# An eight-layer attention stack on one NeuronCore: Wo and W2 products formed token-major at once, biases added from PSUM by VectorE, and another order of work at the opening

## The reference: what is computed

```python
for i in range(B):                       # B = 8 layers, H*K = 1024, F = 1024
    residual = x
    Q = _feature_map(jnp.einsum('nsd,hdk->nshk', x, Wq[i]) + bq[i])   # elu(x) + 1
    Kf = _feature_map(jnp.einsum('nsd,hdk->nshk', x, Wk[i]) + bk[i])
    V = jnp.einsum('nsd,hdk->nshk', x, Wv[i]) + bv[i]
    KV = jnp.sum(Kf * V, axis=1)
    sumK = jnp.sum(Kf, axis=1)
    Z = 1.0 / (Q * sumK[:, None] + 1e-06)
    att = Q * KV[:, None] * Z
    y = jax.nn.gelu(att.reshape(n, s, H * K) @ Wo[i] + bo[i])
    x = _layer_norm(y + residual, ln1_s[i], ln1_b[i])
    residual = x
    h = jax.nn.gelu(x @ W1[i] + b1[i])
    h = jax.nn.gelu(h @ W2[i] + b2[i])
    x = _layer_norm(h + residual, ln2_s[i], ln2_b[i])
```

## Time and profile before

| | us |
|---|---|
| median of 3 runs | 3186.2 (3174.65 to 3186.39) |
| the profiled execution | 3182.43 |
| its span, first to last instruction | 3180.7 |
| TensorE busy (matmuls) | 2953.2 |
| VectorE busy | 2327.8 |
| ScalarE busy | 1890.1 |
| GpSimd busy | 921.6 |

### The profile page before, as it was taken

How to read it: one execution, slowest core, us unless ns; L and a number is a source line. 1 busy time by engine, 2 the same in 40 slices (tenths; PEclk the granted TensorE clock), 3 DMA queues, 4 the chain that set the end, 5 groups by cost and what they waited for, 6 DMA issues and landing times. The chain is left out here.

```text
span 3180.7 us, 36072 instructions
## 1 busy us (share of the span) xinstructions
PE 2953.2 (93%) x11560; PEld 2010.1 (63%) x11561; DVE 2327.8 (73%) x3334; ACT 1890.1 (59%) x2824; POOL 921.6 (29%) x590
## 2 busy tenths in 40 slices
PE   4799999999999999999999999999999969988895
PEld 3566666666656665666666666666666536766563
DVE  7778888888787879788878788878888627752111
ACT  3666677667767776776677667766776614432221
POOL 5004231523151315131513151315131123323002
PEclk8899999999999999999999999999999989988998
DMA  5001101100011001100100010001100010013212
GB/s 128 1 1 23 29 5 32 27 27 17 19 26 27 17 19 26 27 17 20 26 27 17 20 25 27 17 20 26 27 17 4 1 53 1 0 37 134 81 45 76
DMA packets 212241, 92.90 MB, mean 29 GB/s; under 512 B 146792, under 2 KB 207984, under 8 KB 212048
## 3 DMA queue, kind: packets, MB, share of 16 engines
q1 hardware_dynamic: 209408, 83.30, 10.3%
q0 software_dynamic: 2640, 7.21, 0.7%
HBM read 80.24 MB, written 10.22 MB: 28 GB/s over the span
## 5 line engine op out<-in xcount | busy, mean ns | idle before, releaser
L341 PE MATMUL PS<-XTHI,WHI 128*128 128x512 f32 x1536 | 655.0, 426 | 64.5 <-DVE EX L641 44.7
L343 PE MATMUL PS<-XTHI,WLO 128*128 128x512 f32 x1536 | 613.6, 399 | 0.0
L342 PE MATMUL PS<-XTLO,WHI 128*128 128x512 f32 x1536 | 613.3, 399 | 0.0
L269 POOL TENSOR_TENSOR RSTD<-MV,EPS 128x4 f32<-128x4 f32 x68 | 41.2, 606 | 1539.3 <-DVE MV L713 1531.0
L391 PE MATMUL Y<-H,W2S 128*128 128x512 f32 x1024 | 458.1, 596 | 2.7 <-DVE R L703 2.7
L391 PE MATMUL Y<-ATT,WO 128*128 128x512 f32 x1024 | 451.7, 594 | 4.1 <-ACT ATT L540 2.7
L540 ACT ACTIVATE ATT<-INV,CC,CE 128x128 f32<-128x128 f32 x1024 | 425.1, 481 | 3.8 <-DVE INV L687 3.8
L341 PEld LDWEIGHTS PS<-XTHI,WHI 128*128 128x128 f32 x1536 | 294.5, 192 | 157.2 <-issue 67.8
L505 ACT ACTIVATE EX<-PS,BNEG 128x512 f32<-128x512 f32 x256 | 169.9, 686 | 309.5 <-PE PS L343 307.1
L342 PEld LDWEIGHTS PS<-XTLO,WHI 128*128 128x128 f32 x1536 | 294.6, 192 | 83.7 <-issue 20.3
L391 PEld LDWEIGHTS Y<-ATT,WO 128*128 128x128 f32 x1024 | 194.6, 190 | 226.2 <-issue 215.0
(11 more groups left out here) (189 smaller groups left out, 4737.9 us busy)
## 6 DMA issues: line engine op xcount, KB each, us to landing
STAGE<-L_attn_Wk SPq DMA_DIRECT2D x128, 64.0 KB, 2.1
STAGE<-L_attn_Wv SPq DMA_DIRECT2D x128, 64.0 KB, 2.1
STAGE<-L_attn_Wq SPq DMA_DIRECT2D x128, 64.0 KB, 2.1
WO<-L_attn_Wo SPq DMA_DIRECT2D x8, 1024.0 KB, 5.3
W2S<-L_attn_W SPq DMA_DIRECT2D x8, 1024.0 KB, 5.4
STAGE<-L_attn_W SPq DMA_DIRECT2D x64, 128.0 KB, 3.6
RAW<-L_ffn_r_gate SPq DMA_DIRECT2D x8, 512.0 KB
RAW<-L_ffn_r_up SPq DMA_DIRECT2D x8, 512.0 KB
```

What stands on the lines that cost most here:

```text
L341: nc.tensor.matmul(out, whi[:, kc, :], xhi[:, kc, :], start=(kc == 0), stop=False)
L342: nc.tensor.matmul(out, whi[:, kc, :], xlo[:, kc, :], start=False, stop=False)
L343: ins = nc.tensor.matmul(out, wlo[:, kc, :], xhi[:, kc, :], start=False, stop=(kc == KD - 1))
```

## The change

1. `down` swaps its operands. The activations are loaded as stationary operand, 128 tokens at a time, and the 256 columns of the weights stream past. The product has tokens on the partitions at once, in four blocks of 128 tokens. Its blocks are issued (0, 2), (1, 3) for Wo and (0, 1), (2,), (3,) for W2.
2. `to_tm` and its two uses are gone.
3. The biases now lie along the free axis. They are loaded as one row of 256 broadcast to all partitions (`load_row`, in place of `load_fm`). VectorE adds them while it reads `Y` (`biased`, semaphores `y_b` and `z_b`), into `T`.
4. ScalarE's GELU works in place on `T`, one instruction of 128x1024. For y it stands where it stood; for z it stands behind the first hidden GELU. The residual reads `T`.
5. VectorE's addition for y stands between the sums and the tables of pair 1. That for z stands in the sums of pair 3, behind `hidden_lo`. The buffer waits of TensorE (`res1`, `res2`) become `y_b` and `z_b`.
6. At the opening, VectorE makes the low part of the first input before the statistics of the others, and does the normalisations one tile at a time, each behind a pair's tables. GpSimd does the square roots of tiles 1 to 3 together, and waits for the first normalised tile before it splits weights.

The core of the diff, all in `attention_stack` (TensorE, ScalarE, VectorE in this order; the buffers, the loads with `load_row` and the semaphores are left out):

```diff
-            def to_tm(done, value, transposed):
-                pe.wait_ge(done, value)
-                for b in range(TS):
-                    for kc in range(KD):
-                        ins = nc.tensor.transpose(Ytm[:, b, kc * P:(kc + 1) * P], T[:, kc, b * P:(b + 1) * P],
-                                                  ident[:, :])
-                ins.then_inc(transposed, 1)
-            def down(w, src, m, chunks):
-                for c in chunks:
-                    ins = nc.tensor.matmul(Yfm[:, m, :], w[:, c, m * P:(m + 1) * P], src[:, c, :],
-                                           start=(c == 0), stop=(c == HC - 1))
+            def down(w, src, blocks, chunks=range(HC)):
+                for b in blocks:
+                    for c in chunks:
+                        ins = nc.tensor.matmul(Ytm[:, b, :], src[:, c, b * P:(b + 1) * P], w[:, c, :],
+                                               start=(c == 0), stop=(c == HC - 1))
...
                 pair(0, 0, 2, 1)
                 if tile:
                     if at_least(l, t, 2):
-                        pe.wait_ge(res2, g - 1)
+                        pe.wait_ge(z_b, g - 1)
                     if tt == 0:
                         pe.wait_ge(wo_in, (tl + 1) * 16)
                     pe.wait_ge(att, g * PAIRS + 3)
-                    down(WO, ATT, 0, range(HC - 2))
+                    down(WO, ATT, (0, 2), range(HC - 2))
                     pe.wait_ge(att, g * PAIRS + 4)
-                    down(WO, ATT, 0, range(HC - 2, HC))
+                    down(WO, ATT, (0, 2), range(HC - 2, HC))
                 pair(1, 0, 2, 1)
                 if tile:
-                    down(WO, ATT, 1, range(HC)).then_inc(y_mm, 1)
-                pair(2, 0, 2)
-                if tile:
-                    to_tm(y_act, g + 1, yt_mm)
-                pair(2, 1)
+                    down(WO, ATT, (1, 3)).then_inc(y_mm, 1)
+                pair(2, 0, 2, 1)
                 if before:
                     if tile:
-                        pe.wait_ge(res1, g + 1)
+                        pe.wait_ge(y_b, g + 1)
                     else:
-                        pe.wait_ge(res2, g - 1)
+                        pe.wait_ge(z_b, g - 1)
                     if zt == 0:
                         pe.wait_ge(w2_in, (zl + 1) * 16)
                     pe.wait_ge(h_act, g * HC)
-                    down(W2S, H, 0, range(HC))
+                    down(W2S, H, (0, 1))
                 pair(3, 0, 2, 1)
                 if before:
-                    ins = down(W2S, H, 1, range(HC - 3 if tile else HC))
+                    down(W2S, H, (2,))
+                    ins = down(W2S, H, (3,), range(4 if tile else HC))
...
                     if before:
-                        ins = down(W2S, H, 1, range(HC - 3, HC))
+                        ins = down(W2S, H, (3,), range(4, HC))
...
                     hidden(tl, tt, g)
-                if before:
-                    to_tm(z_act, g, zt_mm)
...
-            def gelu_down(mm, bias, bias_in, done, l, t, value):
-                if t == 0:
-                    act.wait_ge(bias_in, (l + 1) * 16)
-                act.wait_ge(mm, value)
-                for m in range(KD):
-                    ins = nc.scalar.activation(T[:, m, :], Yfm[:, m, :], ACT.Gelu_apprx_tanh, bias=bias[:, m:m + 1])
-                ins.then_inc(done, 1)
-            def hidden(l, t, g, between):
+            def gelu_down(biased, done, value):
+                act.wait_ge(biased, value)
+                nc.scalar.activation(T[:, :, :], T[:, :, :], ACT.Gelu_apprx_tanh).then_inc(done, 1)
+            def hidden(l, t, g, between, before):
...
+                    if m == 0 and before:
+                        gelu_down(z_b, z_act, g)
...
                 if tile:
-                    gelu_down(y_mm, BO, bo_in, y_act, tl, tt, g + 1)
+                    gelu_down(y_b, y_act, g + 1)
...
-                if before:
-                    zl, zt = slot_of(l, t - 1)
-                    gelu_down(z_mm, B2, b2_in, z_act, zl, zt, g)
+                if before and not tile:
+                    gelu_down(z_b, z_act, g)
                 if exists(l, t + 2):
                     input_hi(g + 2)
                 if tile:
-                    hidden(tl, tt, g, (nl, nt, 2) if more else None)
+                    hidden(tl, tt, g, (nl, nt, 2) if more else None, before)
...
+                if biased2 is not None:
+                    z_biased(*biased2)
...
+            def biased(mm, value, bias, bias_in, layer, t, free, done):
+                if t == 0:
+                    dve.wait_ge(bias_in, (layer + 1) * 16)
+                if free is not None:
+                    dve.wait_ge(*free)
                 dve.wait_ge(mm, value)
-                nc.vector.tensor_tensor(R[:, w, :, :], Ytm[:, :, :], add, ALU.add).then_inc(res, 1)
+                nc.vector.tensor_tensor(T[:, :, :], Ytm[:, :, :], bcast(bias[:, :], TS), ALU.add).then_inc(done, 1)
+            def residual(w, value, gelu, add, res):
+                dve.wait_ge(gelu, value)
+                nc.vector.tensor_tensor(R[:, w, :, :], T[:, :, :], add, ALU.add).then_inc(res, 1)
...
+            def z_biased(l, t, g, tile):
+                zl, zt = slot_of(l, t - 1)
+                biased(z_mm, g, B2, b2_in, zl, zt, (res1, g + 1) if tile else (res2, g - 1), z_b)
...
                 if old:
-                    residual(w, g - 1, zt_mm, R[:, w, :, :], res2)
+                    residual(w, g - 1, z_act, R[:, w, :, :], res2)
                     statistics(w, g - 1, mv2, res2, 1)
                 if tile:
                     newton(tl, tt, 3)
@@ -743,11 +750,15 @@
                     newton(nl, nt, 0)
                     features(nl, nt, 1)
                     sums_of(nl, nt, 1)
+                if tile:
+                    biased(y_mm, g + 1, BO, bo_in, tl, tt, (res2, g - 1) if old else None, y_b)
+                if more:
                     denominators(nl, nt, 1)
                 if tile:
                     if old:
                         dve.wait_ge(xn, g - 1)
-                    residual(w, g + 1, yt_mm, X[:, tt * TS:(tt + 1) * TS, :], res1)
+                    residual(w, g + 1, y_act, X[:, tt * TS:(tt + 1) * TS, :], res1)
...
-                    sums_of(nl, nt, 3)
+                    sums_of(nl, nt, 3, biased2=(l, t, g, tile) if before else None)
...
             norm_input(0)
+            input_lo(0)
             input_statistics(1)
-            input_lo(0)
             input_statistics(2)
             input_statistics(3)
-            for t in range(1, TILES):
-                norm_input(t)
-            slot(0, -1)
+            for p in range(PAIRS):
+                features(0, 0, p)
+                sums_of(0, 0, p)
+                denominators(0, 0, p)
+                if p < TILES - 1:
+                    norm_input(p + 1)
+                if p < PAIRS - 1:
+                    newton(0, 0, p)
+            input_lo(1)
```

GpSimd at the opening:

```diff
             for k in range(HC):
-                if k % 2 == 0:
-                    t = k // 2
-                    bs = slice(t * TS, (t + 1) * TS)
-                    rstd(RSTD0[:, bs], MV0[:, bs, 1], EPS0, mv0, 2 * t + 2, r0, t + 1)
+                if k == 0 or k == 2:
+                    for t in range(TILES)[:1] if k == 0 else range(1, TILES):
+                        bs = slice(t * TS, (t + 1) * TS)
+                        rstd(RSTD0[:, bs], MV0[:, bs, 1], EPS0, mv0, 2 * t + 2, r0, t + 1)
+                if k == 0:
+                    pool.wait_ge(x0, 1)
```

More of the change, by code:

```diff
@@ L80, in attention_stack @@
         BUP = sb("BUP", [P, 3, HC])
-        BO = sb("BO", [P, KD])
+        BO = sb("BO", [P, D])
         B1 = sb("B1", [P, HC])
-        B2 = sb("B2", [P, KD])
+        B2 = sb("B2", [P, D])
         LN1P = sb("LN1P", [P, 2, D])
@@ L123, in attention_stack @@
             sem(n) for n in ("bo_in", "b1_in", "b2_in", "wo_in", "w2_in", "ln1_in", "ln2_in"))
-        k_mm, v_mm, q_mm, y_mm, yt_mm, x1t_mm, h_mm, z_mm, zt_mm, xt_mm = (
-            sem(n) for n in ("k_mm", "v_mm", "q_mm", "y_mm", "yt_mm", "x1t_mm", "h_mm", "z_mm", "zt_mm", "xt_mm"))
+        k_mm, v_mm, q_mm, y_mm, x1t_mm, h_mm, z_mm, xt_mm = (
+            sem(n) for n in ("k_mm", "v_mm", "q_mm", "y_mm", "x1t_mm", "h_mm", "z_mm", "xt_mm"))
         b_neg, clipped, ex, log, inv, y_act, x1_hi, h_act, z_act, xt_hi = (
@@ L132, in attention_stack @@
             sem(n) for n in ("snap", "kf", "wq", "kv_mul", "sums", "stat", "denom", "residue", "recip", "xt_lo", "x1_lo"))
-        res1, mv1, x0, n1, res2, mv2, n2, mv0 = (
-            sem(n) for n in ("res1", "mv1", "x0", "n1", "res2", "mv2", "n2", "mv0"))
+        y_b, res1, mv1, x0, n1, z_b, res2, mv2, n2, mv0 = (
+            sem(n) for n in ("y_b", "res1", "mv1", "x0", "n1", "z_b", "res2", "mv2", "n2", "mv0"))
         half_set, w_hi, w_lo, r1, r2, xn_s, xn, r0 = (
@@ L185, in load_ln, with load_row @@
```

(17 more changed lines are left out.)

13 lines of the change are left out of this document (6 added, 7 removed).

## The result

The changed kernel takes **3246.1 us** (median of four runs, 3239.0 to 3251.4), the kernel before 3182.7 beside it (3174.7 to 3186.4): ratio 1.020, 95% interval 1.018 to 1.021. The forecast was 3237 with a range of 3174 to 3265, and "slower" had 0.66. The profiled execution has a span of 3249.8 us, against 3180.7 before; the spans are 69.1 us apart.

A forecast was written before the change was run, and what follows sets the result against it. The kernel was taken as balanced: a slot is as long as TensorE's work and as a VectorE-ScalarE chain. 3182.4 + 49 (middle stretch) + 2 (quiet slots) + 10 (clock) - 6 (opening) = 3237 us; range 3174 to 3265.

The forecast's parts named there:

- slower: Whole kernel: time beyond the within-0.5% band, which reached to 3202 us; chance 0.66.
- The middle stretch: End of pair 1's sums to pair 2's features: 11.1 us every slot, +49 over seven layers, +2 for two quiet slots.
- my estimate by that page: ScalarE's table switch, now on the chain: by the page another 1.4 us on 30 slots, result near 3280.
- Transposes worth nothing: TensorE: removing 64 groups of eight transposes, 66.4 us busy time, gains nothing because the chain does not pass through TensorE.
- products for nothing: TensorE: twice as many products, half as wide, cost nothing; two at 0.442 us against one at 0.447.
- Addition and GELU of z: VectorE's b2 addition behind X1LO and ScalarE's GELU are hidden by existing waits: nothing; uncovered, up to 2.3 us a slot.
- Cover under X1LO: TensorE idles about 2 us before input's transposes; lower clock costs 1.5 us in a third of slots: +10, between 0 and +40.
- the head follows TensorE: Rival: without the transposes each slot starts 0.85 us earlier, taking back 26 us, to 3201; chance 0.18.
- Opening: Kernel start: spread normalisations start pair 0's features near 27.6, pair 3's near 81 to 84; -6, between 0 and -15.
- The checks: Expected trace signs: TensorE busy time down some 60 us, quiet slots 76.8 us, longest of a layer near 86.
- TensorE is the bound: Rival: VectorE and ScalarE run ahead, slots shrink by TensorE's work, 38 us, to 3138, up to 3165; chance 0.14.
- The change gives only its opening: Rival: both waits fall on free places, leaving only the opening's -6, 3176 us; chance 0.06.

The follow-up runs named there:

- run 1: Changed kernel with VectorE's addition of y's bias moved ahead of the reduction in the sums of pair 1; 3175.4 us, ratio 0.997.
- Run 7: Changed kernel with VectorE's addition of y's bias moved later, behind the tables of pair 1; 3291.3 us, ratio 1.034.
- run 3: Changed kernel with z's eight transposes put back at each slot's end, results unused; 3245.1 us, ratio 1.019.
- run 8: Changed kernel with six instead of four W2 products behind the turning of x1; 3208.6 us, ratio 1.009.
- run 4: Changed kernel with the old order of work at the opening put back on VectorE and GpSimd; 3251.1 us, ratio 1.021.
- run 6: Kernel before the change, with one W2 product instead of three behind the turning of x1, the other two issued ahead; 3224.0 us, ratio 1.013.

## Why the prediction was right, and where it was not

**The middle stretch, +49 and +2: right, and its reason is shown.** I worked out 11.1 us from durations of the trace before; it measured 11.0 (11.4 in one slot of four). The sum is +49.6 against +51. Runs 1 and 7 moved only the addition, and the stretch went to 8.1 and 13.1. ScalarE's wait turned from the product to VectorE, 7.5 to 7.8 us in three slots of four, where I had said some 8 (10.5 in the fourth). The switch of tables is on the chain now, and still takes 1.28 us, with the next activation 0.02 us behind it (1100.32 to 1101.62). The Trainium skill, "ScalarE: Activation LUTs" (What ACT_TABLE_LOAD costs), adds a drain to each load; my estimate by that page was near 3280. The drain does not show in this trace either.

**Transposes worth nothing, products for nothing: right.** Run 3 puts half of the transposes back, those of z, and the time stays; those of y were not put back. The products cost 5.8 us of 910.

**Addition and GELU of z: nothing.** Both stand behind X1LO, in the third part of the slot. In the quiet slots that are not struck this part lasts 45.0 or 46.3 us, against 45.2 or 46.4 before, so they add nothing there, and TensorE's products into Y wait 1.4 us for additions in the whole kernel (first row of L388 above).

**Cover under X1LO, +10: the mechanism was right, the size was off.** This is the term that was mis-sized. The wait is 2.07 us as predicted, and a struck slot loses 1.64 us by run 8, where I took 1.5. But "if a third of 30 slots pay, less the three that already do", 7 slots, came from three in seven of the earlier trace rows, where the wait is another one. Measured are 21 less 3, 18 slots: 18 x 1.64 = **+29.6**. The forecast came near all the same, in part by luck, because something that it did not contain went the other way: the third part grew by 23.0 only, so the rest of it got 6.6 us shorter. By the traces 4.5 of these 6.6 us lie in the longest slots of six layers (316.2 us in all before, 311.7 in run 8, where no slot is struck), the rest in 0.1 to 0.2 us a slot. That has the sign of my rival "the head follows TensorE", which gave 26, but not its size; and run 3 speaks against its reason, since with z's transposes back the part is as long as in the change. What makes it 6.6 shorter stays open.

**Opening, -6: a little less.** 4.3 us at the first turning of x1, by run 4; the time itself, 5 us, is within the scatter. The features began at 27.31, as worked out (27.6), but those of pair 3 at 85.92 and not at 81 to 84. The step that is off is "a group of normalisations at 6.8, 6.8 and 1.4": these were 5.6, 4.9 and 1.4, even less. Too small was what I took for the rest, three times 12.0 and 2 for GpSimd: it came to 46.7 us. Of the 8.7 us too many, 3.57 are VectorE's wait for ScalarE ahead of the Newton of pair 2, the only wait of this stretch; the others are VectorE's own instructions, longer while GpSimd split weights (the one of L665 took 2.63 us in pair 0 and 1.23 in pair 1).

**The checks.** Quiet slots whose stretch was 10.2 us last 76.5 or 78.1 us, without and with a stretch at the lower clock (76.8 forecast), those whose stretch was 9.06 last 77.8 or 79.4; the longest of a layer 86.1 to 87.6 (near 86). One check failed: TensorE's busy time fell by 15 us and not by some 60. Busy time contains the clock. The hidden products alone took 30.5 us more for the same work.

**The rivals.** "TensorE is the bound" is refuted by run 3 and by the slots, none of which is shorter than 75.5 us in the middle of the stack. "The change gives only its opening" falls with the stretch.

## What to carry to other kernels

A change that hands a step to a second engine (here the bias, from ScalarE's read of PSUM to VectorE) is priced by where that engine stands in its own order when the step comes due: work out the chain from that place, and look at once whether the step can stand one instruction earlier. Here this place decided between 3246 and 3175 us, while 33 us of work on the busiest engine decided nothing. And a wait of TensorE that "costs nothing" should be looked up in the granted clock behind it; where it is followed by the lower level, move independent products into it, but see that no product gets ahead of a step that others wait for (run 6).

## What the runs showed of the hardware

- A wait of 1.9 to 2.1 us on TensorE, ahead of the input's transposes and between stretches of unbroken work, was followed by the lower clock in 19 of 25 slots of the change and in 5 of 8 of run 1. One of 1.2 us (run 8) was so in none of 26, one of 1.55 us (run 6) in none of 21, one of 3.6 us (the change, runs 1 and 7) in 14 of 16, one of 4.5 us (run 6) in 7 of 7. So here the cost of a wait did not go in proportion to its length. The 2.8 us of the kernel before struck three of six times; why that is less often than 2.07, and what decides between two waits of one length, no run tells.
- What the lower clock costs depends on where it falls. At the input's transposes a struck slot lost 1.64 us (run 8). Run 7 spent 174 us at it and the change 123, but its stretches fell mostly on pair 3's products, and the second part of its 30 slots grew by 7.8 us only.
- The fall came alike with a DMA share of 0.74 and of 0.00 (the two windows of the change), and with 0.82 it stayed away (run 6).
